# Even and odd columns and their difference for a 5-tap convolution, with edge values as an own output

## What is computed

```python
s = style @ mw.T + mb
weight = SCALE * w * s[:, None, :, None]
demod = lax.rsqrt(jnp.sum(weight * weight, axis=(2, 3)) + EPS)
weight = weight * demod[:, :, None, None]
```

## Time and profile before

| | |
|---|---|
| median of three runs | 755.43 us (754.4 to 756.1) |
| profiled execution, first to last instruction | 755.1 us |
| TensorE matmuls | 711.5 us busy, 3858 records |
| TensorE weight loads | 622.0 us |
| VectorE | 342.5 us |
| ScalarE | 299.5 us |
| GpSimd | 281.6 us |
| moved by DMA | 108.46 MB |

### The profile page before, as it was taken

One profiled execution on the slowest core, in us unless ns is written; L12 is line 12 of the kernel. 1 busy time (PEld: TensorE's weight loads), 2 busy tenths in 40 slices (PEclk: granted clock), 3 DMA queues, 4 the chain that ended last, 5 costly groups with the idle time before them and its releaser, 6 DMA issues.

```text
span 755.1 us, 10500 instructions
## 1 busy us (share of the span) xinstructions
PE 711.5 (94%) x3858; PEld 622.0 (82%) x3858; DVE 342.5 (45%) x551; ACT 299.5 (40%) x437; POOL 281.6 (37%) x456
## 2 busy tenths in 40 slices
PE   5668999998999999998999999999899999999997
PEld 4557888887888888887888888888788888888886
DVE  5968434435544333445335443453454443334430
ACT  3322444343434344434243444443334444443432
POOL 2431443442333443333443434434334434443310
PEclk9979999999999999999999999999999999999999
DMA  7043267764367767655756666677445777666572
GB/s 253 1 118 64 84 147 175 175 147 118 99 162 175 157 145 166 154 138 115 175 120 155 151 152 148 150 175 175 107 108 137 174 175 170 148 150 164 157 177 83
DMA packets 112162, 108.46 MB, mean 144 GB/s; under 512 B 4528, under 2 KB 78640, under 8 KB 112112
## 3 DMA queue, kind: packets, MB, share of 16 engines
q1 hardware_dynamic: 111456, 106.22, 58.6%
q10 hardware_dynamic: 656, 1.57, 0.6%
HBM read 36.47 MB, written 33.55 MB: 93 GB/s over the span
## 4 chain that ended last, share of the span: by engine, by line
PE 77%; DVE 10%; issue 6%; POOL 3%; ACT 2%; DMA 1%; POOLq 0%; ACTq 0%; DVEq 0%
PE po L159 16%; PE po L161 16%; PE po L160 16%; PE pg L159 7%; PE pg L161 6%; PE pg L160 6%; PE pg L164 3%; PE pg L165 3%; POOL Q2l L520 2%; DVE xl L595 1%; DVE Wf L617 1%; DVE Q2f L606 1%; POOL Q2h L168 1%; ACT Q2h L418 1%; ACT W L428 1%
## 5 line engine op out<-in xcount | busy, mean ns | idle before, releaser
L159 PE MATMUL po<-xh,W 128*128 128x512 f32 x640 | 254.5, 398 | 0.0
L160 PE MATMUL po<-xl,W 128*128 128x512 f32 x640 | 253.4, 396 | 0.0
L161 PE MATMUL po<-xh,W 128*128 128x512 f32 x640 | 253.4, 396 | 0.0
L595 DVE TENSOR_TENSOR xl<-X,xh 128x1032 fp32r<-128x1032 f32 x64 | 81.8, 1277 | 201.3 <-ACT xh L396 201.1
L403 ACT ACTIVATE T<-po,cv,DD 128x512 f32<-128x512 f32 x128 | 99.7, 779 | 169.2 <-PE po L161 167.7
L161 PEld LDWEIGHTS po<-xh,W 128*128 128x128 f32 x640 | 125.2, 196 | 24.5
L159 PEld LDWEIGHTS po<-xh,W 128*128 128x128 f32 x640 | 125.8, 197 | 20.6 <-issue 0.2
L160 PEld LDWEIGHTS po<-xl,W 128*128 128x128 f32 x640 | 125.6, 196 | 20.1
L520 POOL TENSOR_TENSOR Q2l<-Q2f,Q2h 128x512 fp32r<-128x512 f32 x31 | 40.0, 1290 | 228.3 <-ACT Q2h L418 228.3
L428 ACT CAST W<-Wf 128x512 fp32r<-128x512 f32 x64 | 46.6, 728 | 119.3 <-DVE Wf L617 93.0
L613 DVE TENSOR_TENSOR Gf<-pg,D10c 128x512 f32<-128x512 f32 x64 | 44.0, 689 | 103.8 <-PE pg L165 103.6
(11 more groups left out here) (154 smaller groups left out, 998.2 us busy)
## 6 DMA issues: line engine op xcount, KB each, us to landing
X<-in_xin SPq DMA_DIRECT2D x64, 516.0 KB, 5.3
out<-T SPq DMA_DIRECT2D x64, 512.0 KB, 3.1
W<-W SPq DMA_DIRECT2D x96, 256.0 KB, 6.6
W<-W SPq DMA_DIRECT2D x32, 384.0 KB, 7.6
E<-in_ed ACTq DMA_DIRECT2D x1, 768.0 KB, 8.5
XE<-in_xe SPq DMA_DIRECT2D x1, 576.0 KB, 11.1
Gf<-in_mwt SPq DMA_DIRECT2D x1, 256.0 KB, 3.2
A2f<-in_a ACTq DMA_DIRECT2D x1, 256.0 KB, 6.3
```

The source lines that it names most:

```text
L159: eng.matmul(o, wh_, rh, start=first, stop=False)
L160: eng.matmul(o, wh_, rl, start=False, stop=False)
L161: return eng.matmul(o, wl_, rh, start=False, stop=last)
L595: tt(xl[:, n % XH], X[:, n % XR], r32(xh[:, n % XH]), ALU.subtract).then_inc(s_xl, 1)
```

## The change

A sample's 512 columns are taken as 256 even and 256 odd ones. With A the taps 0, 2 and 4 on the even columns and B the taps 1 and 3 on the odd ones, the even outputs are A + B. With D(m) = odd(m) - even(m+1), the odd outputs are A(m+1) + B(m) + (W0 - W1) D(m) + (W2 - W3) D(m+1) + W4 D(m+2). That is eight tap products of 256 columns instead of five of 512.

- TensorE: per sample `conv_even(b)` into bank ps, `conv_diff(b - 1)`, which accumulates on the bank of its B, and `conv_odd(b)`. In the tile names pb is the B bank, ps the A bank.
- ScalarE evicts A and B to a new buffer AB of three slots (`a_out`, `b_out`). It casts 1548 columns of x a pair instead of 1032, and W in three parts of 768, 1024 and 512 elements instead of two of 512 and 768.
- GpSimd forms the difference columns (`columns`) and the even outputs (`even_out`). The copies of edge values into T go; they leave as an own output, and the host puts them in place.
- VectorE forms the tap differences (`w_diff`), lows of three parts of W, lows of 1548 columns of x, and the odd outputs (`odd_out`).
- SP: six crossing DMAs a group instead of four. X has three slots instead of four, xh and xl two instead of three, T two instead of three.
- Units (1,2) and (1,3) move into the prologue, and `SLOTS` puts units 0 and 1 last. Edge steps are spread over all groups, one for two groups.

```diff
-L2 = 512
-XW = L2 + 4
+H = 256
+XW = H + 2
...
-XR = 4
-XH = 3
-TR = 3
+XR = 3
+XH = 2
+TR = 2
+AR = 3
 NP = 4
-ND = 2
+NX = 6
...
-SLOTS = [[(1, 4), (1, 5), (1, 6)], [(2, 0), (2, 1)], [(2, 2)], [(2, 3)]]
+PROLOGUE = [(0, 0), (0, 1), (0, 2), (0, 3), (1, 0), (1, 1), (0, 4), (0, 5), (0, 6), (1, 2), (1, 3)]
+FIRST = [[(1, 4), (1, 5), (1, 6)], [(2, 0), (2, 1)], [(2, 2)], [(2, 3), (3, 0), (3, 1)]]
+SLOTS = [[(1, 4), (1, 5), (1, 6)], [(2, 2)], [(2, 3)], [(3, 0), (3, 1)]]
+C0, C1, W0, W1, W2, W3, W4, C3, C2, ZB = range(10)
+PARTS = [slice(C1, W1 + 1), slice(W2, C3 + 1)]
+OUTER = slice(C0, C2 + 1, C2 - C0)
...
-            def cross(g, part):
+            def cross(g, k):
                 w = r32(W[:, g % 2])
...
+                sp.wait_ge(s_wh, 3 * g + k + 1)
+                sp.wait_ge(s_wl, 3 * g + k + 1)
+                if k < 2:
+                    v = slice(PARTS[k].start - C1, PARTS[k].stop - C1)
+                    sp.dma_start(w[hi, v, :, :, 1], w[lo, v, :, :, 0]).then_inc(s_w[g % 2], 16)
+                    a, e = (W0, W1) if k == 0 else (W1, W4)
+                    sp.dma_start(w[lo, a + 1 - C1:e + 1 - C1, :, :, 1], w[hi, a - C1:e - C1, :, :, 0]).then_inc(s_w[g % 2], 16)
+                else:
+                    for v, j in enumerate((C1, C3)):
+                        sp.dma_start(w[lo, j - C1, :, :, 1], r32(M[hi, v])).then_inc(s_w[g % 2], 16)
...
             for g in range(NGR):
                 n = NG // Q * g
                 if n + XR < NQ:
                     load(n + XR)
                 if n:
                     store(n - 1)
+                if g + 1 < NGR:
+                    for k in range(3):
+                        cross(g + 1, k)
                 if n + 1 + XR < NQ:
                     load(n + 1 + XR)
-                if g + 1 < NGR:
-                    cross(g + 1, 0)
-                    cross(g + 1, 1)
                 store(n)
...
-            def conv(b):
+            def taps(b, o, e, js, onto=False):
+                g, i = divmod(b, NG)
+                n, q = divmod(b, Q)
+                for k, (j, start, stop) in enumerate(js):
+                    w = [W[:, g % 2, j - C1, t, i // 2].rearrange("p r (o b) -> p (r o) b", b=2)[:, :, i % 2]
+                         for t in range(2)]
+                    m = split_mm(pe, o, w[0], w[1], xh[:, n % XH, q, e, k:k + H], xl[:, n % XH, q, e, k:k + H], start, stop, onto)
+                return m
+            def conv_even(b):
                 g, i = divmod(b, NG)
                 n, q = divmod(b, Q)
                 if i == 0:
...
+                    pe.wait_ge(s_wh, 3 * g + 2)
+                    pe.wait_ge(s_wl, 3 * g + 2)
+                    pe.wait_ge(s_w[g % 2], 16 * NX * (g // 2 + 1))
                 if q == 0:
                     pe.wait_ge(s_xh, n + 1)
                     pe.wait_ge(s_xl, n + 1)
+                if b:
+                    pe.wait_ge(s_ae, b)
+                taps(b, pa, 0, ((W0, True, False), (W2, False, False), (W4, False, True))).then_inc(s_a, 1)
+            def conv_odd(b):
                 if b >= 2:
-                    pe.wait_ge(s_t, b - 1)
...
+                    pe.wait_ge(s_yo, b - 1)
+                taps(b, pb[b % 2][:, 0:H], 1, ((W1, True, False), (W3, False, True))).then_inc(s_b, 1)
+            def conv_diff(b):
+                pe.wait_ge(s_be, b + 1)
+                taps(b, pb[b % 2][:, 0:H], 2, ((C1, False, False), (C3, False, False), (W4, False, True)),
+                     True).then_inc(s_p, 1)
...
-                conv(b)
-                if divmod(b, NG) in edge_at:
-                    edge(*edge_at[divmod(b, NG)])
+                conv_even(b)
+                if b:
+                    conv_diff(b - 1)
+                conv_odd(b)
+                if i == 3 and g % 2 == 0:
+                    edge(*divmod(g // 2, 4))
+            conv_diff(B - 1)
...
+                act.wait_ge(s_s, n + 1)
                 if n >= XH:
-                    act.wait_ge(s_o, Q * (n - XH + 1))
+                    act.wait_ge(s_p, Q * (n - XH + 1))
...
+            def a_out(b):
+                act.wait_ge(s_a, b + 1)
+                if b >= AR:
+                    act.wait_ge(s_ye, b - AR + 1)
+                    act.wait_ge(s_yo, b - AR + 1)
+                act.activation(AB[:, b % AR, 0, 0:H], pa, ACT.Identity,
+                               bias=cv[:, b:b + 1], scale=DD[:, 3, b:b + 1]).then_inc(s_ae, 1)
+            def b_out(b):
+                act.wait_ge(s_b, b + 1)
+                act.mul(AB[:, b % AR, 1, 0:H], pb[b % 2][:, 0:H], DD[:, 3, b:b + 1]).then_inc(s_be, 1)
...
+            def w_high(g, k):
+                act.wait_ge(s_cd, 2 * g + min(k, 1) + 1)
+                if k < 2:
+                    if g >= 2:
+                        act.wait_ge(s_p, NG * (g - 1))
+                    act.copy(taps_of(g, 0, k), Wf[:, :, PARTS[k]]).then_inc(s_wh, 1)
                 else:
...
+                    if g:
+                        act.wait_ge(s_w[(g - 1) % 2], 16 * NX * ((g - 1) // 2 + 1))
+                    act.copy(outer_of(0), Wf[hi, :, OUTER]).then_inc(s_wh, 1)
...
-                if b:
-                    t_out(b - 1)
-                if b % Q == 0 and b // Q + 2 < NQ:
-                    x_high(b // Q + 2)
+                n = (b + 1) // Q
+                if b % Q == 1 and XH <= n < NQ:
+                    x_high(n)
+                if i == 1 and g + 3 < NGR:
+                    q3_high(g + 3)
+                if i == 0:
+                    a_out(b)
                 for x in units_of(b):
-                    if x[1] != 5:
+                    if x[1] == 4:
+                        for k in range(3):
+                            w_high(x[0], k)
+                    elif x[1] < 4:
                         high(*x)
-                if i == 3 and g + 3 < NGR:
-                    q3_high(g + 3)
...
+            def columns(n):
+                pool.wait_ge(s_x[n % XR], 16 * (n // XR + 1))
+                if n == XR - 1:
+                    pool.memset(X[:, n, :, 2, XW - 1:XW], 0.0)
+                x = X[:, n % XR]
+                pool.tensor_tensor(x[:, :, 2, 0:XW - 1], x[:, :, 1, 0:XW - 1], x[:, :, 0, 1:XW], ALU.subtract).then_inc(s_s, 1)
+            def even_out(b):
+                n, q = divmod(b, Q)
+                pool.wait_ge(s_ae, b + 1)
+                pool.wait_ge(s_be, b + 1)
+                if q == 0 and n >= TR:
+                    pool.wait_ge(s_st[n % TR], 16 * (n // TR))
+                ab = AB[:, b % AR]
+                pool.tensor_tensor(T[:, n % TR, q, 0], ab[:, 0, 0:H], ab[:, 1, 0:H], ALU.add).then_inc(s_ye, 1)
...
-                if i == 0 and g + 1 < NGR:
-                    identity(g + 1)
+                if b:
+                    even_out(b - 1)
+                n = b // Q + 1
+                if b % Q == 0 and XH <= n < NQ:
+                    columns(n)
+                if i == 0 and g + 3 < NGR:
+                    q3_full(g + 3)
                 for x in units_of(b):
                     if x[1] < 4:
                         low(*x)
-                if i == 2 and g + 3 < NGR:
-                    q3_full(g + 3)
-                if i == 3 and g + 3 < NGR:
+                if i == 1 and g + 3 < NGR:
                     q3_low(g + 3)
-                if b % Q == 1 and b > Q:
-                    finish(b // Q - 1)
-            finish(NQ - 1)
+                if i == 3 and g + 2 < NGR:
+                    identity(g + 2)
+            even_out(B - 1)
...
+            def w_diff(g, k):
+                if k == 0:
+                    dve.wait_ge(s_ce, cnt(g, 4))
+                    tt(Wf[:, :, C0:C1 + 1], Wf[:, :, ZB:C1:W0 - ZB], Wf[:, :, W0:W1 + 1], ALU.subtract).then_inc(s_cd, 1)
                 else:
...
-            def w_low(g, part):
...
+                    dve.wait_ge(s_ce, cnt(g, 6))
+                    tt(Wf[:, :, C2:W4:-1], Wf[:, :, W1:W2 + 1], Wf[:, :, W2:W3 + 1], ALU.subtract).then_inc(s_cd, 1)
+            def w_low(g, k):
+                dve.wait_ge(s_wh, 3 * g + k + 1)
+                if k < 2:
+                    m = tt(taps_of(g, 1, k), Wf[:, :, PARTS[k]], r32(taps_of(g, 0, k)), ALU.subtract)
+                else:
+                    if g:
+                        dve.wait_ge(s_w[(g - 1) % 2], 16 * NX * ((g - 1) // 2 + 1))
+                    m = tt(outer_of(1), Wf[hi, :, OUTER], r32(outer_of(0)), ALU.subtract)
+                m.then_inc(s_wl, 1)
+            def odd_out(b):
+                n, q = divmod(b, Q)
+                dve.wait_ge(s_ae, b + 1)
+                dve.wait_ge(s_p, b + 1)
+                if q == 0 and n >= TR:
+                    dve.wait_ge(s_st[n % TR], 16 * (n // TR))
+                dve.scalar_tensor_tensor(out=T[:, n % TR, q, 1], in0=pb[b % 2][:, 0:H], scalar=DD[:, 3, b:b + 1],
+                                         in1=AB[:, b % AR, 0, 1:H + 1], op0=ALU.mult, op1=ALU.add).then_inc(s_yo, 1)
...
+            link(dve.memset(AB[:, :, 0, H:H + 1], 0.0))
+            full(1, 2)
```

(24 more changed lines are left out.)

176 lines of the change are left out of this document (83 added, 93 removed).

## The result

The changed kernel takes 758.69 us (median of 12 runs, 756.59 to 759.76), the kernel before 756.3 beside it (12 runs, 753.75 to 758.42): ratio 1.0036, interval 1.0022 to 1.005. It is slower by a little more than can be told apart, where 728.5 was forecast: outside the forecast's own 705 to 750, inside the wide range of 692 to 770. The profiled execution spans 757.2 us, so 28.7 us of the sum are missing.

The account below looks back on a forecast made before the run. TensorE's stream was taken as the bound, with VectorE next to critical. 51.7 (prologue) + 588.5 (loop work) + 59 (stalls) + 20 (edges) + 5 (last group, ring) + 4.3 (end) = 728.5 us; own range 705 to 750, wide range 692 to 770.

Parts of the forecast that it names:

- The stream of TensorE: TensorE's loop matmuls: 256-column ones 0.120 us apart, loop work 588.5 us, 18.2 us a group.
- the stall before unit 2: TensorE's once-a-group wait for GpSimd's lows of Q2, most of 32 us of stalls before; expected to go.
- The 81 us of the convolution: TensorE's convolution: 24 matmuls of 256 columns replace 15 of 512, saving 0.63 us a sample, 81 us in all.
- First, the x ring: Two-slot x ring: VectorE's x low waits for diff, then TensorE waits; about 0.6 us a group with restart.
- My walk gives 1.3: VectorE and GpSimd excluding each other: walking one group's operations in order gave 1.3 us added delay per group.
- 11.6 us + 1.3: VectorE's run from odd output to x low: 11.6 us back-to-back, plus 1.3 us of exclusion delay.
- the bounds of 0 and 3.7: Added exclusion delay per group: 0 if VectorE and GpSimd never meet, 3.7 us if GpSimd fits only beside PSUM reads.
- TensorE's clock unchanged: Expected sign in the profile after: TensorE's granted clock stays as before, with 256-column matmuls 0.120 us apart.
- Edges, 20 us: Edge steps on VectorE behind the odd output: about 5 us a chunk, times 4, 20 us of delay.
- Crossings: SP's crossing DMAs: 1.66 MB need 8.5 us a group, hidden with 3 us in hand.
- Prologue and ends: Outside the steady loop: 51.7 us ahead, 5 us for last group and bare ring, 4.3 us behind the last matmul.
- the one in which the exclusion becomes the bound: Rival 2: VectorE and GpSimd exclusion sets the pace, 22.1 us a group, 774 us, slower than before; chance 0.17.

Follow-up runs that it names:

- The third slot: Changed kernel with three slots of xh and xl instead of two (raw x two instead of three), x lows moved to VectorE's idle stretches: 761.16 us, ratio 1.0056.
- e7: Changed kernel with all 16 edge steps left out on VectorE and TensorE: 721.9 us, ratio 0.953.
- e5: Changed kernel with ScalarE's b_out of a group's first sample between first and second W high instead of behind all three: 770.26 us, ratio 1.0162.

## Why the prediction was wrong

- *The stream of TensorE*: right. 256-column matmuls stand 0.120 apart, 586.7 us of work against 585.9, and the stall before unit 2 went (two waits of TensorE name GpSimd's Q2, 5.4 us in all). The 81 us of the convolution were won.
- *"First, the x ring"*: the mechanism is the one that runs, with TensorE's leg 6.7 us where 6.2 was taken. The third slot shows that it is not the only loop near this length.
- *"My walk gives 1.3"*: this is the step that failed, the delay that the exclusion adds to a group. VectorE's unbroken run was taken as 11.6 us + 1.3 and is 14.1. In the rows of e7 the exclusion adds 0.87 to one x low (2.63 against 1.76), 0.65 to the second tap difference (1.34 against 0.69), 0.4 to the two W lows (2.52 against 2.11, their sum where they meet nothing, in the three-slot kernels), 0.33 to M low and 0.29 to the identity add: 2.55 us, between the bounds of 0 and 3.7 but not near the lower end. In the changed kernel itself the means of these forms give 2.2 us a group. The odd outputs add 3 x 0.07. (The 11.6 is not what its terms make at 0.07 less each, 12.0 - 1.05; the rows less their meetings give some 11.3.) In the sum this makes a group 21.6 us (18.2 + 0.6 + 2.55 + 0.2) instead of 20.1, against 20.80 measured without edges. The measured 0.7 on 31 groups are 22 of the 28.7 us. The table agrees: without edges, waits and restarts are 86.5 us where the sum had 62.
- *"TensorE's clock unchanged"*: failed. The sum had 2 us for one slow stretch ahead of the loop and nothing in it; 14.2 us go at half clock in eight stretches, seven of which are not there without the edges. These 13.0 us don't come on top of the rest: they stand in for most of the waits that the sum took for the edges. The kernel before has four such stretches in its loop, which the sum did not count apart from the stalls.
- *The hand-over of the odd sum* was not in the sum. By the starts TensorE waits 18.7 us for it. Taking it away in e5 won nothing: the wait came back before the even products (3.35 us for 1.86 and 1.40). What it costs by itself no run shows.
- *Edges, 20 us*: right in sum (36.8 with TensorE's 15.7 in it, against 35.7), wrong in kind. Beside TensorE's own, 8.5 us are waits and restarts and 13 the half clock behind them, 21.5 together, and the greater part can be had back by cutting the steps (14 us).
- *Crossings*: hidden, as said. No wait of TensorE names them.
- *Prologue and ends*: within 1 us.
- *The rivals*: the one in which the exclusion becomes the bound decided from 20.8 us a group; without edges the group is 20.80, and with them 21.95 ((737.74 - 57.20) / 31). Its 774 was too high by the edges, which it priced apart on top. It was the nearest in time, and 0.17 was too little for it. Its mechanism is only half what happened: the group is not as long as the sum of what the two engines exclude, but as the chain of the forecast with more meetings in VectorE's run. That its group of 22.1 us lies beside the 21.95 with edges is chance.

## What to carry to other kernels

When two engines become three quarters busy and exclude each other, don't walk one group for the meetings: take the engine's unbroken run in the loop that closes, and charge every exclusive operation in it with a meeting until a trace says otherwise. Price a wait of TensorE by its length and not by the sum, and look for two waits with little work between them: cut what stands before them in one piece, and don't join short waits that lie apart. Put what feeds TensorE ahead of what waits for TensorE in a queue.

## What the hardware showed beyond that

TensorE's granted clock went from 2.4 GHz to 1.2 behind waits of about 2 us, single ones and pairs, in a stream that was busy 86% overall, and each such fall cost 1.5 to 2.6 us (17 to 28 matmuls at some 0.21 instead of 0.12). The Trainium skill (TensorE: Matmul & The Clock Gate, Part 1) calls the throttled state the default one, which activity releases. The rows agree in that the half clock came behind waits and went while TensorE was busy; which state is the default they do not show. They show that a loop with waits pays for it many times (eight here). An output of 256 columns that VectorE reads from PSUM, with a second input in SBUF, took 0.476 to 0.481 us in the mean in the changed kernel and in each experiment, while with both inputs in SBUF the second tap difference went from 0.69 us to 1.34 and the identity add from 0.42 up to 1.40.
